# Roots of the query and key norms: from GpSimd's power and a three-round iteration to ten VectorE operations

## Chip, cores and metric

The kernel runs on one core of one Trainium2 chip. The metric is the device time of one execution in microseconds (us).

## What is computed

A transformer block for 16 sequences of 128 tokens with 128 features: a modulated linear layer, causal attention with 16 query heads and 4 key heads of 8 features (weights made ternary), a residual, an LSTM over the 128 tokens, a quantised feed-forward layer and a second residual. The part that the change touches is the root-mean-square norm of every query and key head:

```python
def rms_norm(x):
    eps = jnp.asarray(jnp.finfo(x.dtype).eps, x.dtype)
    return x * jax.lax.rsqrt(jnp.mean(x * x, axis=-1, keepdims=True) + eps)
...
q, k = (rms_norm(q), rms_norm(k))
...
q = q * q_gain.astype(q.dtype)[None, None, :, None]
...
x = x + _L0_attn_ref(_L0_cond_ref(x, cond_1024, L0_cond_weight), ...)
x = x + _L0_ffn_ref(_L0_cond2_ref(x, cond_1024, L0_cond2_Wx, L0_cond2_Wh, L0_cond2_b), ...)
```

## The kernel before

The 128 tokens of every sequence are cut into four blocks of 32 tokens. Attention goes block by block; the LSTM goes token by token, in 128 steps. The attention of block 0 and part of that of block 1 is done ahead of the LSTM's first step (the prologue); the rest of blocks 1 to 3 is spread over the steps by tables written by hand (`..._AT`, lines 392 to 434): step t of every engine ends with `side(t)`, which issues what the tables have for t. All engines run their own instruction list in order and wait for each other by counting semaphores.

One LSTM step is a ring: TensorE adds the products with the hidden state (line 1343), ScalarE takes tanh of the gates (line 958), VectorE makes the cell (`prod`, line 1846, and line 1849), ScalarE takes tanh of the cell (line 963), VectorE makes the hidden state in two parts (`h_hi`, line 1854, `h_lo`, line 1858), and TensorE begins the next step. VectorE's side work stands between `h_lo` of one step and `prod` of the next; TensorE's stands behind the products of the next step.

The norm of a block needs the sums of squares of 8 features for 80 columns (4 tiles of 20 heads) on 128 partitions (`sum_squares`, line 1562), and then 1/sqrt of mean plus epsilon, times the gain. It is made in two ways:

- Blocks 0 and 1, in the prologue, on VectorE (`head_norm`, lines 1564 to 1586): 13 operations, each of which waits for the one before: scale and epsilon, a shift and a subtraction on the bits as a first guess, three rounds of three operations, the gain.
- Blocks 2 and 3 on GpSimd (`head_norms`, lines 522 to 533): scale and epsilon, a power with exponent -0.5 (line 529), the gain. Block 2's stands between `row_norms(0)` and `max_parts(1, 0)`, block 3's between `max_parts(2, 1)` and `max_parts(2, 2)`.

`max_parts(k, u)` (lines 548 and 550) writes the maxima of the scores (`neg_max`, line 1632, VectorE) into the stack `m_stack`, from which TensorE's `lowered_queries` (lines 1088 and 1091) makes lowered queries; TensorE does so for tile 2 of block 2 in step 38. The roots are used by `scale_heads` (line 1609): in the prologue for blocks 0 and 1, in step 14 for block 2 and in step 46 for block 3.

In the prologue GpSimd makes identity and masks; it waits for VectorE (line 1708), takes the power for the modulation (line 566), makes the masks, fills the places of the values (`v_1`, which the trace names `v`, and `v_all`, lines 587 to 590), makes `gate_pick` and fills paddings. Behind VectorE's root of block 1 stand the ten operations of `ternary(PROJ_C, n)` (lines 1499 to 1523).

Of the kernel before, what the change touches and what calls it, by code (L numbers as in the profile page):

```python
# [23 lines left out]


def adaln_attention_lstm_ffn(nc, xT, condT, cond_w, w_qkv, w_proj, q_gain, Wx, Wh, b, clip_x,
# [4 lines left out]
    HD = D // HEADS  # L31
# [23 lines left out]
    with ExitStack() as ctx:  # L55
# [3 lines left out]
        def sem(name):  # L59
            return ctx.enter_context(nc.semaphore(name))  # L60
# [452 lines left out]
        def _(gp):  # L513
# [3 lines left out]
            def then(ins):  # L517
                made[0] += 1
                ins.then_inc(pool, 1)
                gp.wait_ge(pool, made[0])  # L520

            def head_norms(k):

                c, n = k % 2, QK_POOL_OPS * (k - 2)
                gp.wait_ge(squares_summed, 2 * k + 2)
                G.tensor_scalar(qk_r[:, c, 1, :], qk_r[:, c, 1, :], 1.0 / HD, FP32_EPS, ALU.mult, ALU.add).then_inc(qk_pool, 1)
                gp.wait_ge(qk_pool, n + 1)
                gp.wait_ge(rotated, 2 * (k - 1))
                G.tensor_tensor(qk_r[:, c, 0, :], qk_r[:, c, 1, :], minus_half[:, :].broadcast_to([P, TILES * NH]), ALU.pow).then_inc(qk_pool, 1)  # L529
                gp.wait_ge(qk_pool, n + 2)  # L530
                gp.wait_ge(gain_ready, 1)
                r = qk_r[:, c, 0, :].rearrange("p (t h) -> p t h", t=TILES)[:, :, 0:HEADS]
                G.tensor_tensor(r, r, gain_n[:, :].unsqueeze(1).broadcast_to([P, TILES, HEADS]), ALU.mult).then_inc(qk_pool, 1)

            def row_norms(k):
# [17 lines left out]
            def normalise_0(T):  # L553
# [31 lines left out]
            gp.wait_ge(masks, 1)  # L585

            then(G.memset(v_1[:, :, :, :], 0.0))
            then(G.memset(v_1[:, :, :, HD], 1.0))
            then(G.memset(v_all[:, :, :, :], 0.0))
            G.memset(v_all[:, :, :, HD], 1.0).then_inc(v_pads, 1)  # L590
# [408 lines left out]
        def _(pe):  # L999
# [465 lines left out]
        def _(v):  # L1465
# [98 lines left out]
            def head_norm(k, n):  # L1564


                c = k % 2
                x, y, tmp = qk_r[:, c, 1, :], qk_r[:, c, 0, :], qk_r[:, c, 2, :]
                if n == 0:
                    v.wait_ge(squares_summed, 2 * k + 2)  # L1570
                    V.tensor_scalar(x, x, 1.0 / HD, FP32_EPS, ALU.mult, ALU.add).then_inc(qk_link, 1)
                    return
                v.wait_ge(qk_link, QK_OPS * k + n)
                if n == 1:
                    V.tensor_scalar(tmp.bitcast(I32), x.bitcast(I32), 1, None, ALU.logical_shift_right).then_inc(qk_link, 1)
                elif n == 2:
                    V.tensor_scalar(y.bitcast(I32), tmp.bitcast(I32), -1.0, float(0x5F3759DF), ALU.mult, ALU.add).then_inc(qk_link, 1)
                elif n > NEWTON:
                    r = y.rearrange("p (t h) -> p t h", t=TILES)[:, :, 0:HEADS]
                    V.tensor_tensor(r, r, gain_n[:, :].unsqueeze(1).broadcast_to([P, TILES, HEADS]), ALU.mult).then_inc(qk_link, 1)  # L1580
                elif n % 3 == 0:
                    V.tensor_tensor(tmp, y, y, ALU.mult).then_inc(qk_link, 1)
                elif n % 3 == 1:
                    V.scalar_tensor_tensor(out=tmp, in0=tmp, scalar=-0.5, in1=x, op0=ALU.mult, op1=ALU.mult).then_inc(qk_link, 1)
# [17 lines left out]
            def scale_heads(k, h):  # L1602
                v.wait_ge(turned_qk, 2 * k + h + 1)
                if k < 2:
                    v.wait_ge(qk_link, QK_OPS * (k + 1))
                else:
                    v.wait_ge(qk_pool, QK_POOL_OPS * (k - 1))
# [179 lines left out]
            def side(t):  # L1787
# [3 lines left out]
                for k in range(1, BLOCKS):  # L1791
# [177 lines left out]
```

## Time and profile before

| what | us |
| --- | --- |
| median of 3 runs | 347.69 |
| the runs | 342.56, 348.14, 347.69 |
| span of the profiled execution | 345.6 |
| TensorE busy in it | 281.5 |
| VectorE busy | 230.0 |
| ScalarE busy | 179.6 |
| GpSimd busy | 71.8 |

The profiled execution has a span, from its first to its last instruction; its device time apart from the span isn't listed. The median lies 2.1 us above this span and the fastest run 3.0 us below it. The times of rows are us from the start of the span. A row of a timeline says: start, length, engine, line, operation, output <- input, shape; in brackets the idle time of the engine just before it, and what ended it.

### The profile page before, as it was taken

What the parts mean: (1) busy time and instruction counts of PE and PEld (TensorE: products, weight loads), DVE (VectorE), ACT (ScalarE), POOL (GpSimd) and SP (SyncE); (2) the same over time, 40 slices, a digit from 0 to 9 for tenths busy, and PEclk for the clock granted to TensorE, in tenths of its full rate; (3) what the DMA queues carried; (4) which work ended last, traced back from release to release, by engine and by line L of the source; (5) the groups of instructions that cost most, each with busy time, mean ns of one, the idle gap of its engine ahead of it and who ended that gap; (6) DMA issues with size and microseconds to landing.
All of it is one profiled execution on the core that took longest, in us unless ns stands there. A gap on an engine that the chain in (4) does not pass through costs nothing.

```text
span 345.6 us, 9250 instructions
## 1 busy us (share of the span) xinstructions
PE 281.5 (81%) x3509; PEld 175.5 (51%) x3510; DVE 230.0 (67%) x1077; ACT 179.6 (52%) x560; POOL 71.8 (21%) x95
## 2 busy tenths in 40 slices
PE   6949859898989789799988899997787887856243
PEld 2426544686757457576555676654444344321010
DVE  4686894758687777476578667545666565556866
ACT  7343953745466776556544555445225223249670
POOL 2731338700001039300020000001000000005624
PEclk9998996776598975555858756569999989996955
DMA  5600000000000000000000000000000000000003
GB/s 111 166 1 2 4 2 0 2 5 2 2 4 2 2 2 3 0 3 3 2 2 2 3 2 1 2 3 2 0 3 2 1 3 2 0 2 1 0 0 121
DMA packets 3773, 4.04 MB, mean 12 GB/s; under 512 B 1169, under 2 KB 2449, under 8 KB 3729
## 3 DMA queue, kind: packets, MB, share of 16 engines
q1 hardware_dynamic: 3360, 3.28, 3.5%
q8 instruction: 28, 0.46, 0.6%
q10 hardware_dynamic: 368, 0.16, 0.2%
q14 instruction: 17, 0.13, 0.1%
HBM read 2.40 MB, written 1.05 MB: 10 GB/s over the span
## 4 chain that ended last, share of the span: by engine, by line
PE 46%; DVE 26%; ACT 15%; issue 6%; POOL 4%; DMA 1%; ACTq 0%; DVEq 0%; POOLq 0%
PE bank L1343 14%; ACT tanh_c L963 4%; DVE prod L1846 4%; PE bank L1245 4%; PE bank L1407 4%; ACT gates_sb L958 4%; POOL qk_r L529 4%; DVE gates_sb L1849 4%; DVE h_hi L1854 4%; PE bank L1164 3%; PE bank L1252 3%; DVE neg_max L1632 2%; PE bank L1110 2%; PE bank L1199 2%; PE bank L1187 2%
## 5 line engine op out<-in xcount | busy, mean ns | idle before, releaser
L958 ACT ACTIVATE gates_sb<-bank 128x64 f32<-128x64 f32 x128 | 28.5, 223 | 73.3 <-PE bank L1343 70.9
L1343 PEld LDWEIGHTS bank<-h_hi,wh_hi 128*128 128x128 f16 x508 | 25.3, 103 | 71.5 <-DVE h_hi L1854 64.5
L1407 PE MATMUL bank<-ident_b,zero_w 128*128 128x512 bf16 x171 | 55.6, 422 | 0.0
L1846 DVE SCALAR_TENSOR_TENSOR prod<-gates_sb 128x32 f32<-128x32 f32 x128 | 24.7, 193 | 46.1 <-ACT gates_sb L958 43.2
L1343 PE MATMUL bank<-h_hi,wh_hi 128*128 128x16 f16 x508 | 34.4, 177 | 24.7 <-DVE h_hi L1854 24.0
L963 ACT ACTIVATE tanh_c<-gates_sb 128x16 f32<-128x16 f32 x128 | 27.6, 216 | 40.3 <-DVE gates_sb L1849 37.3
L1854 DVE TENSOR_TENSOR h_hi<-o_scaled,tanh_c 128x16 f16<-128x16 f32 x128 | 22.5, 176 | 25.3 <-ACT tanh_c L963 25.2
L1343 PE MATMUL bank<-h_lo,wh_hi 128*128 128x16 f16 x508 | 32.8, 174 | 0.1
L759 ACT ACTIVATE probs<-bank,gain_max 128x512 f32<-128x512 f32 (+1 forms) x44 | 29.4, 675 | 6.6 <-PE bank L1119 6.0
L1245 PE MATMUL bank<-x1T,wx_sb 128*128 128x128 f32 x128 | 32.2, 367 | 0.0
L1343 PE MATMUL bank<-h_hi,wh_lo 128*128 128x16 f16 x508 | 31.5, 171 | 0.0
L1632 DVE TENSOR_REDUCE neg_max<-bank 128x4 f32<-128x384 f32 (+3 forms) x44 | 27.7, 636 | 1.4 <-PE bank L1077 1.4
L529 POOL TENSOR_TENSOR qk_r<-qk_r,minus_half 128x80 f32<-128x80 f32 x2 | 26.2, 13106 | 0.2
L635 POOL TENSOR_TENSOR h_ffn<-xT_sb 96x512 f32<-96x512 f32 (+1 forms) x8 | 10.0, 1263 | 77.6 <-ACT xT_sb L985 77.6
L1858 DVE TENSOR_TENSOR h_lo<-hidden,h_hi 128x16 f16<-128x16 f32 x128 | 22.4, 175 | 4.4
L1849 DVE SCALAR_TENSOR_TENSOR gates_sb<-prod 128x16 f32<-128x16 f32 x128 | 22.4, 175 | 4.4
L1343 PEld LDWEIGHTS bank<-h_lo,wh_hi 128*128 128x128 f16 x508 | 22.0, 100 | 2.0 <-DVE h_lo L1858 0.2
L1252 PE MATMUL bank<-zero_w 128*128 128x512 bf16 x65 | 21.8, 493 | 1.2 <-DVE one L1688 1.2
L1245 PEld LDWEIGHTS bank<-x1T,wx_sb 128*128 128x128 f32 x128 | 22.5, 236 | 0.4 <-issue 0.4
L1343 PEld LDWEIGHTS bank<-h_hi,wh_lo 128*128 128x128 f16 x508 | 22.4, 99 | 0.0
L1856 DVE TENSOR_TENSOR hidden<-o_scaled,tanh_c 128x16 f32<-128x16 f32 x128 | 21.5, 168 | 0.1
L1851 DVE TENSOR_SCALAR o_scaled<-gates_sb 128x16 f32<-128x16 f32 x128 | 21.5, 168 | 0.0
(245 smaller groups left out, 520.6 us busy)
## 6 DMA issues: line engine op xcount, KB each, us to landing
xT_sb<-xT SPq DMA_DIRECT2D x4, 256.0 KB, 4.9
outT<-probs SPq DMA_DIRECT2D x4, 256.0 KB, 2.7
wh_sb<-Wh SPq DMA_DIRECT2D x1, 256.0 KB, 2.7
wx_sb<-Wx SPq DMA_DIRECT2D x1, 256.0 KB, 5.4
ffn_nat<-w_down SPq DMA_DIRECT2D x1, 176.0 KB, 3.6
ffn_nat<-w_gate SPq DMA_DIRECT2D x1, 128.0 KB, 3.7
ffn_nat<-w_up SPq DMA_DIRECT2D x1, 128.0 KB, 3.5
w_nat<-w_qkv ACTq DMA_DIRECT2D x1, 64.0 KB, 1.9
```

Of the source, the lines that this page charges most:

```text
L529: G.tensor_tensor(qk_r[:, c, 0, :], qk_r[:, c, 1, :], minus_half[:, :].broadcast_to([P, TILES * NH]), ALU.pow).then_inc(qk_pool, 1)
L759: A.activation(probs[0:keys, n % 2, g, :], bank[COL_BANKS[k][g]][0:keys, :], ACT.Exp, scale=gain_max[0:keys, 2:3]).then_inc(probs_ready, 1)
L958: A.activation(gates_sb[:, now, 0:GATES * B], bank[(t // BANK_STEPS) % 2][:, slot:slot + GATES * B], ACT.Tanh, scale=scale).then_inc(gates ...
L963: A.activation(tanh_c[:, :], gates_sb[:, nxt, GATES * B:], ACT.Tanh, scale=0.5).then_inc(tanh_done, 1)
L1245: return E.matmul(out, wx_sb[:, g * P:(g + 1) * P], x1T[:, chunk * BANK_STEPS:(chunk + 1) * BANK_STEPS, :], start=False, stop=False, skip_ ...
L1252: E.matmul(bank[dst][:, :], zero_w[:, :], zero_w[:, :].unsqueeze(1).broadcast_to([P, 4, P]), start=not keep, stop=not keep, skip_group_che ...
L1343: ins = E.matmul(bank[dst][:, col:col + B], w[:, g * P:(g + 1) * P], h[:, part, :], start=False, stop=True, skip_group_check=True)
L1407: E.matmul(bank[1 - ((t + 1) // BANK_STEPS) % 2][:, :], zero_w[:, :], ident_b[:, :].unsqueeze(1).broadcast_to([P, 4, P]), start=False, sto ...
L1632: V.tensor_reduce(neg_max[:, per * u:per * (u + 1), g], bank[ROW_BANKS[k][g]][:, 0:per * keys].rearrange("p (b k) -> p b k", b=per), AX.X, ...
L1846: V.scalar_tensor_tensor(out=prod[:, :], in0=G[:, now, 0:2 * B], scalar=1.0, in1=G[:, now, 3 * B:5 * B], op0=ALU.add, op1=ALU.mult).then_i ...
L1849: V.scalar_tensor_tensor(out=G[:, nxt, 4 * B:5 * B], in0=prod[:, B:2 * B], scalar=0.5, in1=prod[:, 0:B], op0=ALU.mult, op1=ALU.add).then_i ...
L1854: V.tensor_tensor(h_hi[:, now, :], o_scaled[:, :], tanh_c[:, :], ALU.mult).then_inc(hidden_hi, 1)
```

## The change

All four blocks take the root on VectorE with ten operations: one fewer for the first guess and two rounds instead of three, the second of them of higher order, with the gain multiplied in between (it waits for nothing new). Block 0 and block 1 do the ten in the prologue. Blocks 2 and 3 do two of the ten per LSTM step, block 2 in steps 0 to 4, block 3 in steps 33 to 37; `sum_squares` of block 3 stays in step 32. GpSimd's `head_norms` is gone. The four fills of `v_1` and `v_all` stand ahead of the power of the modulation; `gate_pick` gets a semaphore of its own.

```diff
+ROOT_A, ROOT_B, ROOT_S = 0.703952253, 2.38924456, 0.375
...
-        NEWTON = 11
-        QK_OPS = NEWTON + 2
-        QK_POOL_OPS = 3
+        QK_OPS = 10
...
+        NORMS_AT = {2: tuple(n // 2 for n in range(QK_OPS)), 3: tuple(33 + n // 2 for n in range(QK_OPS))}
...
-            def head_norms(k):
-
-                c, n = k % 2, QK_POOL_OPS * (k - 2)
-                gp.wait_ge(squares_summed, 2 * k + 2)
-                G.tensor_scalar(qk_r[:, c, 1, :], qk_r[:, c, 1, :], 1.0 / HD, FP32_EPS, ALU.mult, ALU.add).then_inc(qk_pool, 1)
-                gp.wait_ge(qk_pool, n + 1)
-                gp.wait_ge(rotated, 2 * (k - 1))
-                G.tensor_tensor(qk_r[:, c, 0, :], qk_r[:, c, 1, :], minus_half[:, :].broadcast_to([P, TILES * NH]), ALU.pow).then_inc(qk_pool, 1)
...
+            then(G.memset(v_1[:, :, :, :], 0.0))
+            then(G.memset(v_1[:, :, :, HD], 1.0))
+            then(G.memset(v_all[:, :, :, :], 0.0))
+            G.memset(v_all[:, :, :, HD], 1.0).then_inc(v_pads, 1)
             gp.wait_ge(demod_eps, 1)
             G.tensor_tensor(demod[:, 0, :], demod[:, 1, :], minus_half[:, :].broadcast_to([P, B]), ALU.pow).then_inc(demod_ready, 1)
...
-            head_norms(2)
             max_parts(1, 0)
...
-            head_norms(3)
             for u in range(2, UNITS[2]):
...
+                after = (0, 1, 2, 3, 4, 5, 6, 6, 7, 9)[n]
                 if n == 0:
                     v.wait_ge(squares_summed, 2 * k + 2)
...
+                else:
+                    v.wait_ge(qk_link, QK_OPS * k + after)
+                if n == 0:
+                    ins = V.tensor_scalar(x, x, 1.0 / HD, FP32_EPS, ALU.mult, ALU.add)
+                elif n == 1:
+                    ins = V.tensor_scalar(y.bitcast(I32), x.bitcast(I32), -0.5, float(0x5F1FFFF9), ALU.mult, ALU.add)
                 elif n == 2:
+                    ins = V.tensor_tensor(tmp, y, y, ALU.mult)
+                elif n == 3:
+                    ins = V.scalar_tensor_tensor(out=tmp, in0=tmp, scalar=-ROOT_A * ROOT_S, in1=x, op0=ALU.mult, op1=ALU.mult)
+                elif n == 4:
+                    ins = V.scalar_tensor_tensor(out=y, in0=tmp, scalar=ROOT_A * ROOT_B * ROOT_S, in1=y, op0=ALU.add, op1=ALU.mult)
+                elif n == 5:
+                    ins = V.scalar_tensor_tensor(out=tmp, in0=y, scalar=1.0 / (ROOT_S * ROOT_S), in1=y, op0=ALU.mult, op1=ALU.mult)
+                elif n == 6:
+                    ins = V.tensor_tensor(tmp, tmp, x, ALU.mult)
+                elif n == 7:
...
+                    ins = V.tensor_tensor(r, r, gain_n[:, :].unsqueeze(1).broadcast_to([P, TILES, HEADS]), ALU.mult)
+                elif n == 8:
+                    ins = V.scalar_tensor_tensor(out=tmp, in0=tmp, scalar=-10.0 / 3.0, in1=tmp, op0=ALU.add, op1=ALU.mult)
                 else:
+                    ins = V.scalar_tensor_tensor(out=y, in0=tmp, scalar=5.0, in1=y, op0=ALU.add, op1=ALU.mult)
+                ins.then_inc(qk_link, 1)
...
+                        for n in range(QK_OPS):
+                            if t == NORMS_AT[k][n]:
+                                head_norm(k, n)
```

GpSimd's list in the prologue, before, from the clearing of `diag_w` on (the masks follow it, and behind them the four fills of lines 587 to 590):

```order
L564 MEMSET diag_w 128x224
L566 TENSOR_TENSOR demod<-demod,minus_half 128x16
L570 AFFINE_SELECT diag_w<-diag_w 128x128 x4
L572 MEMSET mask_rows 128x32
L573 MEMSET mask_cols 128x32
```

And the same place after the change:

```order
L550 MEMSET diag_w 128x224
L551 MEMSET v 128x1024
L552 MEMSET v 128x32
L553 MEMSET v_all 128x2048
L554 MEMSET v_all 128x64
L556 TENSOR_TENSOR demod<-demod,minus_half 128x16
L560 AFFINE_SELECT diag_w<-diag_w 128x128 x4
L562 MEMSET mask_rows 128x32
L563 MEMSET mask_cols 128x32
```

The four fills have moved from behind the masks to the place ahead of the power of `demod`.

GpSimd's list from the maxima of block 2's second unit on, before:

```order
L550 TENSOR_TENSOR m_stack<-neg_max,m_stack 128x16
L526 TENSOR_SCALAR qk_r<-qk_r 128x80
L529 TENSOR_TENSOR qk_r<-qk_r,minus_half 128x80
L533 TENSOR_TENSOR qk_r<-qk_r,gain_n 128x4x16
L548 CAST m_stack<-neg_max 128x16
L550 TENSOR_TENSOR m_stack<-neg_max,m_stack 128x16
L548 CAST m_stack<-neg_max 128x16
L550 TENSOR_TENSOR m_stack<-neg_max,m_stack 128x16
L537 TENSOR_SCALAR rms_y<-y_sum 128x4
```

And after the change:

```order
L536 TENSOR_TENSOR m_stack<-neg_max,m_stack 128x16
L534 CAST m_stack<-neg_max 128x16
L536 TENSOR_TENSOR m_stack<-neg_max,m_stack 128x16
L534 CAST m_stack<-neg_max 128x16
L536 TENSOR_TENSOR m_stack<-neg_max,m_stack 128x16
L523 TENSOR_SCALAR rms_y<-y_sum 128x4
```

The three operations of block 3's root, the power among them, no longer stand between the second and the third unit's maxima.

VectorE's list at the end of LSTM step 3 and the start of step 4, before (`neg_max` is the side work of the step):

```order
L1858 TENSOR_TENSOR h_lo<-hidden,h_hi 128x16
L1632 TENSOR_REDUCE neg_max<-bank 128x8
L1846 SCALAR_TENSOR_TENSOR prod<-gates_sb 128x32
L1849 SCALAR_TENSOR_TENSOR gates_sb<-prod 128x16
L1851 TENSOR_SCALAR o_scaled<-gates_sb 128x16
```

And after the change:

```order
L1852 TENSOR_TENSOR h_lo<-hidden,h_hi 128x16
L1624 TENSOR_REDUCE neg_max<-bank 128x8
L1571 TENSOR_TENSOR qk_r<-qk_r 128x80
L1576 TENSOR_TENSOR qk_r<-qk_r,gain_n 128x4x16
L1840 SCALAR_TENSOR_TENSOR prod<-gates_sb 128x32
L1843 SCALAR_TENSOR_TENSOR gates_sb<-prod 128x16
L1845 TENSOR_SCALAR o_scaled<-gates_sb 128x16
```

Two operations of block 2's root stand between the side work of the step and `prod` of the next; the other nine pairs stand in the same place of their steps.

## Rows read from the trace of the kernel before

**Rows 1.** The page: clock by 40 slices; the chain by engine and line.
```profile
PEclk9998996776598975555858756569999989996955
...
PE 46%; DVE 26%; ACT 15%; issue 6%; POOL 4%; DMA 1%; ACTq 0%; DVEq 0%; POOLq 0%
```

**Rows 2.** Waits of TensorE, 20 to 60 us: total, times, longest.
```profile
PE bank L1056 <- DVE wmax L1738: 4.4, 1, 4.4
```

**Rows 3.** Timeline of VectorE, 15 to 26 us: block 0's root.
```profile
17.39 1.69 DVE L1571 TENSOR_SCALAR qk_r<-qk_r 128x80 f32<-128x80 f32 x1
...
22.17 0.23 DVE L1580 TENSOR_TENSOR qk_r<-qk_r,gain_n 128x64 f32<-128x64 f32 x1
22.65 0.89 DVE L1599 TENSOR_TENSOR rot<-rot,sin_part 128x320 f32<-128x320 f32 x2 [0.26 <-issue]
```

**Rows 4.** Timeline of POOL (GpSimd), prologue.
```profile
1.56 0.28 POOL L564 MEMSET diag_w<- 128x224 bf16 x1
7.48 2.96 POOL L566 TENSOR_TENSOR demod<-demod,minus_half 128x16 f32<-128x16 f32 x1 [5.63 <-DVE demod L1708]
...
15.99 0.95 POOL L587 MEMSET v<- 128x1024 f32 x1
...
17.22 1.80 POOL L589 MEMSET v_all<- 128x2048 f32 x1
19.08 0.20 POOL L590 MEMSET v_all<- 128x64 f32 x1
```

**Rows 5.** Timeline of VectorE, 36.7 to 44.7 us: block 1's root and what follows.
```profile
37.70 0.20 DVE L1571 TENSOR_SCALAR qk_r<-qk_r 128x80 f32<-128x80 f32 x1
...
38.41 0.24 DVE L1582 TENSOR_TENSOR qk_r<-qk_r 128x80 f32<-128x80 f32 x1
...
40.89 0.23 DVE L1580 TENSOR_TENSOR qk_r<-qk_r,gain_n 128x64 f32<-128x64 f32 x1
41.03 1.20 DVE L1499 CAST tw_b<-w_nat 128x128 bf16<-128x128 f32 x1
```

**Rows 6.** Timeline of POOL (GpSimd), later.
```profile
40.99 1.16 POOL L613 TENSOR_TENSOR wh_lo<-wh_sb,wh_hi 128x512 f16<-128x512 f32 x1 [2.70 <-ACT wh_hi L851]
...
53.45 13.11 POOL L529 TENSOR_TENSOR qk_r<-qk_r,minus_half 128x80 f32<-128x80 f32 x1
...
75.34 0.32 POOL L548 CAST m_stack<-neg_max 128x32 f16<-128x32 f32 x1 [8.39 <-DVE neg_max L1632]
...
127.56 13.11 POOL L529 TENSOR_TENSOR qk_r<-qk_r,minus_half 128x80 f32<-128x80 f32 x1
```

**Rows 7.** Timeline of PE (TensorE), 121 to 146 us: the wait in step 38.
```profile
141.67 0.60 PE L1088 MATMUL bank<-ident_h,q_stack 128*128 128x128 f16 x4 [1.75 <-POOL m_stack L550]
```

**Rows 8.** Timeline of VectorE in steps 1, 2, 4, 35 and 37.
```profile
63.26 0.42 DVE L1627 COPY qT<-bank 128x512 f16<-128x512 f16 x1
63.95 0.19 DVE L1846 SCALAR_TENSOR_TENSOR prod<-gates_sb 128x32 f32<-128x32 f32 x1 [0.27 <-ACT gates_sb L958]
...
67.61 0.19 DVE L1846 SCALAR_TENSOR_TENSOR prod<-gates_sb 128x32 f32<-128x32 f32 x1
...
131.55 0.19 DVE L1846 SCALAR_TENSOR_TENSOR prod<-gates_sb 128x32 f32<-128x32 f32 x1 [0.16 <-ACT gates_sb L958]
...
136.38 0.55 DVE L1632 TENSOR_REDUCE neg_max<-bank 128x4 f32<-128x384 f32 x1
```

**Rows 9.** Timeline of PE (TensorE), 0 to 64 us: products with zeros.
```profile
15.94 5.34 PE L1252 MATMUL bank<-zero_w 128*128 128x512 bf16 x24
...
27.22 1.48 PE L1252 MATMUL bank<-zero_w 128*128 128x512 bf16 x3
...
52.07 4.43 PE L1252 MATMUL bank<-zero_w 128*128 128x512 bf16 x10
```

**Rows 10.** Instructions of line 1846, 110 to 125 us and 126 to 139 us.
```profile
L1846 DVE SCALAR_TENSOR_TENSOR prod<-gates_sb x8: 191/192/194, 111.1 to 123.4; 128x32 f32<-128x32 f32 x8
...
L1846 DVE SCALAR_TENSOR_TENSOR prod<-gates_sb x6: 192/193/329, 127.6 to 137.1; 128x32 f32<-128x32 f32 x6
```

More of the change, by code:

```diff
@@ L211, in adaln_attention_lstm_ffn @@
         masks = sem("masks")
+        picks = sem("picks")
         pads = sem("pads")
@@ L237, in adaln_attention_lstm_ffn @@
         qk_link = sem("qk_link")
-        qk_pool = sem("qk_pool")
         cos_0 = sem("cos_0")
@@ L364, in adaln_attention_lstm_ffn @@
         Y_OPS = 2
-        NEWTON = 11
-        QK_OPS = NEWTON + 2
-        QK_POOL_OPS = 3
+        QK_OPS = 10
         PADS = 4 + TB
-        MASKS = 1 + PARTS
         LIN_BANKS = (4, 4, 4, 3)
@@ L520, in then @@
                 gp.wait_ge(pool, made[0])
-            def head_norms(k):
-                c, n = k % 2, QK_POOL_OPS * (k - 2)
-                gp.wait_ge(squares_summed, 2 * k + 2)
-                G.tensor_scalar(qk_r[:, c, 1, :], qk_r[:, c, 1, :], 1.0 / HD, FP32_EPS, ALU.mult, ALU.add).then_inc(qk_pool, 1)
-                gp.wait_ge(qk_pool, n + 1)
-                gp.wait_ge(rotated, 2 * (k - 1))
-                G.tensor_tensor(qk_r[:, c, 0, :], qk_r[:, c, 1, :], minus_half[:, :].broadcast_to([P, TILES * NH]), ALU.pow).then_inc(qk_pool, 1)
[L530 to L533, printed above, removed]
             def row_norms(k):
@@ L585, in _ @@
             gp.wait_ge(masks, 1)
[L587 to L590, printed above, removed]
             then(G.memset(gate_pick[:, :, :], 0.0))
@@ L593, in _ @@
                 G.affine_select(out=gate_pick[:, :, :], in_=gate_pick[:, :, :], compare_op=ALU.not_equal, fill=1.0,
-                                base=-GATES * part, pattern=[[-1, GATES], [0, B]], channel_multiplier=1).then_inc(masks, 1)
-                gp.wait_ge(masks, 2 + part)
+                                base=-GATES * part, pattern=[[-1, GATES], [0, B]], channel_multiplier=1).then_inc(picks, 1)
+                gp.wait_ge(picks, 1 + part)
             then(G.memset(ffn_nat[I_LAST:P, 0:2, (IC - 1) * P:IC * P], 1.0))
@@ L1313, in _ @@
             project_qkv(2, 1)
-            pe.wait_ge(masks, MASKS)
+            pe.wait_ge(picks, PARTS)
             pe.wait_ge(biasT_ready, 1)
@@ L1568, in head_norm @@
                 x, y, tmp = qk_r[:, c, 1, :], qk_r[:, c, 0, :], qk_r[:, c, 2, :]
+                after = (0, 1, 2, 3, 4, 5, 6, 6, 7, 9)[n]
                 if n == 0:
                     v.wait_ge(squares_summed, 2 * k + 2)
[L1571 to L1575, printed above, removed]
-                elif n == 2:
-                    V.tensor_scalar(y.bitcast(I32), tmp.bitcast(I32), -1.0, float(0x5F3759DF), ALU.mult, ALU.add).then_inc(qk_link, 1)
-                elif n > NEWTON:
-                    r = y.rearrange("p (t h) -> p t h", t=TILES)[:, :, 0:HEADS]
[L1580 to L1584, printed above, removed]
-                else:
-                    V.scalar_tensor_tensor(out=y, in0=tmp, scalar=1.5, in1=y, op0=ALU.add, op1=ALU.mult).then_inc(qk_link, 1)
@@ new lines, in head_norm @@
+                else:
[4 more added lines that the diff above has]
+                    ins = V.tensor_scalar(y.bitcast(I32), x.bitcast(I32), -0.5, float(0x5F1FFFF9), ALU.mult, ALU.add)
+                elif n == 2:
+                    ins = V.tensor_tensor(tmp, y, y, ALU.mult)
[8 more added lines that the diff above has]
+                elif n == 7:
+                    if k == 0:
+                        v.wait_ge(gain_ready, 1)
+                    r = y.rearrange("p (t h) -> p t h", t=TILES)[:, :, 0:HEADS]
+                    ins = V.tensor_tensor(r, r, gain_n[:, :].unsqueeze(1).broadcast_to([P, TILES, HEADS]), ALU.mult)
+                elif n == 8:
+                    ins = V.scalar_tensor_tensor(out=tmp, in0=tmp, scalar=-10.0 / 3.0, in1=tmp, op0=ALU.add, op1=ALU.mult)
+                else:
+                    ins = V.scalar_tensor_tensor(out=y, in0=tmp, scalar=5.0, in1=y, op0=ALU.add, op1=ALU.mult)
@@ L1603, in scale_heads @@
                 v.wait_ge(turned_qk, 2 * k + h + 1)
[L1604 to L1607, printed above, removed]
+                v.wait_ge(qk_link, QK_OPS * (k + 1))
                 n = half(h)
@@ L1728, in _ @@
             turn_sin_0()
-            v.wait_ge(gain_ready, 1)
             head_norms(0)
```

## The prediction

> **What bounds the kernel now.** I read the page first, then the waits of TensorE in the prologue, then the timelines of VectorE and GpSimd around the two kinds of root, and last TensorE's timeline where it waits for GpSimd. The page's chain runs through TensorE for 46% of the span and VectorE for 26%; GpSimd has 4%, about 14 us, which is one long piece of it [rows 1]. In the prologue VectorE is what is waited for: TensorE idles 4.4 us ahead of block 0's transposes until VectorE has come through its list [rows 2], and block 0's root stands in that list. In the LSTM steps the ring through four engines bounds the time; side work costs only where it outlasts the gap that the ring leaves on its engine. GpSimd's power takes 13.11 us twice [rows 6]. The second one is the 4% of the chain: TensorE stands still for 1.75 us in step 38 until the maxima queued behind that power are in `m_stack` [rows 7].
>
> **Price of one root operation.** Block 1's root shows them undisturbed: three scalar operations from 37.70 to 38.41, 0.24 us each from start to start; nine with two inputs from 38.41 to 40.89, 0.276 each; and the gain, behind which an operation that doesn't wait for it begins after 0.14 [rows 5]. Together 3.33 us from 37.70 to 41.03. The new ten: two scalar operations, 0.47; the four that make guess and square, 4 x 0.276 = 1.10; then the product with x (n = 6), in whose shadow the gain goes, 0.28; the next, 0.28; and 0.15 until the work behind the last can begin. That is 2.28, so an undisturbed root is 1.05 us shorter.
>
> One rule speaks against the short gaps. The row of the gain shows 0.23 us of length and the next start after 0.14 [rows 5]. The Trainium skill, "VectorE: DVE Perf Modes", section "The DRAIN you can't avoid", says that the next operation doesn't start until the pipe is empty, with or without a semaphore. By that rule the gain wouldn't hide and every pair in a step would cost about 0.1 us more, a microsecond in all; the row disagrees with it, and the sum goes by the row.
>
> **Block 0, on the path.** Here the first operation lasts 1.69 us instead of 0.20 [rows 3, 5]. It begins at 17.39, while GpSimd's fill of `v_all` runs from 17.22 to 19.02, and ends at 19.08, just behind that fill [rows 4]. The fills move to the front: `diag_w` ends at 1.84 and the power waits for VectorE until 7.48 [rows 4]; the four fills, which now run from 15.99 to 19.28 = 3.29 us, would end at about 5.1, with 2.3 us to spare, so the power isn't late. What GpSimd does at 17.4 then is `gate_pick` and paddings, short pieces. Root 0 lasts 5.26 from 17.39 to 22.65, 0.26 of it an idle piece with no releaser [rows 3]. After: 2.28, plus the idle piece, plus 0.2 for a short collision, is 2.74. Saved: 2.5. The bounds: 1.05 if something else on GpSimd holds the first operation as long as now, 2.98 if neither collision nor idle piece is left. I take the value near the upper one, as the fill that held it is gone. TensorE's wait of 4.4 us has room for all of it [rows 2].
>
> The row of the held operation ends 0.06 us behind the fill [rows 3, 4]. The Trainium skill, "SBUF — State Buffer", section "Who interferes with whom", says that VectorE's scalar operations can take a pair of ports shared with GpSimd, whoever comes second being blocked for the whole instruction. By this rule the 1.49 us over the undisturbed length go with the fill, as in the 2.5; without it the operation may be slow for a reason of its own, and 1.05 is left.
>
> **Block 1, on the path.** The root is 1.05 shorter. Behind it the cast of line 1499 takes 1.20, beginning at 41.03 beside GpSimd's `wh_lo`, 40.99 to 42.15 [rows 5, 6]. `wh_lo` follows ScalarE, whose work doesn't get shorter here, so VectorE comes to the cast a microsecond ahead of it. The cast goes through, and one of the next scalar operations, three to five places behind, meets `wh_lo` instead. I count the stall as moved, not gone: 1.0 saved in all, between 0.2 (a stall that is worse placed) and 2.0 (no stall left).
>
> **Block 2, steps 0 to 4.** Removing its power from GpSimd gives nothing: the maxima behind it wait 8.39 us for VectorE anyway [rows 6]. On VectorE a dependent pair costs 0.276 + 0.15 = 0.43, an independent one 0.29. In step 1 the gap behind the copy of `qT` is 0.27 idle [rows 8], so 0.16 shows; step 2 is like it. The pair of step 3 stands ahead of `prod` at 67.61, which has no idle before it [rows 8], so 0.29 shows at most; in steps 0 and 4 I find wider gaps. That is 0.6 on VectorE; TensorE has work of its own at that point and takes the state late anyway, so I count half, 0.3 (bounds 0 and 0.6).
>
> **Block 3, steps 33 to 37.** The power goes, and TensorE's 1.75 us go with it [rows 7]: the last maximum of that unit is made at 136.38 to 136.93 [rows 8], GpSimd's two short pieces take 0.6, and TensorE asks at 139.9. Even 1.0 us of delay in these steps leaves slack; the bound on the other side is 0.9, if half of the stall returns as a wait for `h_hi`. Against this, four of the five pairs follow a maximum, and step 35's `prod` comes after 0.16 idle [rows 8]: 3 x (0.43 - 0.16) + (0.29 - 0.16) = 0.94 on VectorE. TensorE runs at the lower of its levels there (below) and is the slower engine, so I count 0.4 (bounds 0 and 0.94).
>
> **The sum.** -2.5 - 1.0 + 0.3 - 1.75 + 0.4 = -4.55, about -4.6 us. The profiled span of 345.6 would become 341.0. What lies around the span isn't shown; the median of the runs is 2.1 above it, and I keep that: 347.69 - 4.6 = 343.1 us, 1.3% less. The measurement of this kernel can tell about 2% from no change; its three runs alone differ by 5.6 us.
>
> **The rivals.**
>
> *The clock stays up (faster).* The granted clock is near full in the first slices, dips in the fourth, and is 0.6 in the seventh [rows 1]. The same products with zeros cost 0.22 us each at 15.94, 0.49 at 27.22 and 0.44 at 52.07 [rows 9], so both later groups ran at or near 1.2 GHz and the first at 2.4 GHz. The dip at 27 follows the 4.4 us of idle TensorE [rows 2]; with the root 2.5 us earlier that idle time is 1.9. If neither dip comes, 3 x 0.27 + 10 x 0.22 = 3.0 us go as well: -7.6, 340.1 us. For it: the idle stretch more than halves. Against it: TensorE still has thin stretches ahead of 52, and the idle piece doesn't vanish.
>
> *The prologue's gain is hidden (same).* If TensorE's own zeros or ScalarE take over as the limit behind root 0, only step 38 pays: -1.75 + 0.7 = -1.05, 346.6 us. Against it: the 4.4 us [rows 2] and VectorE's list without an idle mark around root 1 [rows 5].
>
> *The pairs feed the low clock (slower).* A step takes (123.4 - 111.1)/7 = 1.76 us in the stretch before the clock falls and (137.1 - 127.6)/5 = 1.90 behind it [rows 10], in the four slices at 0.5 [rows 1]. If the pairs in steps 33 to 37 make TensorE wait for the state, so that it stays at 1.2 GHz through the rest of block 3's steps, each step costs 0.14 more. From 4.6/0.14 = 33 more low steps on the gain is gone; with 50 (steps 39 to 88) the time is 343.1 + 7.0 = 350.1 us. For it: the clock is already low for four slices here. Against it: a standstill of 1.75 us goes from the same stretch.
>
> **Chances.** Forecast 0.55, clock up 0.25, hidden 0.12, low clock 0.08. The forecast's own range is 340.9 to 345.1: with the better ends of all terms (0.5, 1.0 and 0.7) 2.2 us more go; with all worse ends (1.45, 0.8, 0.3, 0.54 and 0.9) 4.0 come back, of which I take half, since they don't come together. The wider range takes in the fast rival with the better ends, 340.1 - 2.2 = 337.9, and on the other side the hidden gain plus the 2.1 by which I set the median above the span, 348.7. Faster by over 2% means below 340.7: nearly all of the clock rival and a little of the forecast, 0.27. Slower by over 2% means above 354.6: 0.02. The rest, 0.71, lies within 2%.
>
> **What would show it.** Block 0's first root operation at 0.2 to 0.5 us instead of 1.69, and 2.3 to 2.8 us from it to the next line; the power of `demod` still at about 7.5 us; `prod` of step 1 at about 60.4 instead of 63.95 [rows 8]; the wait of TensorE for `m_stack` in step 38 gone; steps 33 to 37 within 0.2 us of what they take now. I am wrong if the first operation is still held, if step 1 starts less than 2 us earlier, if the pairs lengthen steps by 0.4 us and more, or if the clock's low slices move to where they cost more than the terms save.

## The result and the profile after

The changed kernel takes 334.49 us (median of 4 runs, 332.46 to 337.59); the kernel before, beside it on the same chip, 345.62 (342.56 to 348.14). The ratio is 0.9691, 95% interval 0.9595 to 0.9786: some 11 us less, where 4.6 were forecast, and below both ranges of the forecast (340.9 and, with the rivals, 337.9 at the fast end). Of 16 runs of the changed kernel in three sessions the median is 335.4, of 59 of the kernel before 345.6, so about 10 us is the gain to explain. Medians here are of all runs; ratios and their intervals are of the runs in the faster of two states alone. The profiled execution has a span of 333.5 us and a device time of 335.35; what lies around the span is 1.8 us.

The page of the changed kernel, the clock by 40 slices and the chain by engine:

```profile
PEclk9999958796997855556955775599999999995755
...
PE 46%; DVE 28%; ACT 16%; issue 6%; POOL 2%; DVEq 0%; ACTq 0%; POOLq 0%
```

Against [rows 1] GpSimd's share of the chain has halved, from 4% to 2%. The fourth slice stands at 9 instead of 8; the first low slice is the sixth, at 5, where it was the seventh, at 6. VectorE's two roots and what follows the second:

```profile
15.82 0.21 DVE L1559 TENSOR_SCALAR qk_r<-qk_r 128x80 f32<-128x80 f32 x1
...
17.59 0.22 DVE L1576 TENSOR_TENSOR qk_r<-qk_r,gain_n 128x64 f32<-128x64 f32 x1
17.73 0.23 DVE L1578 SCALAR_TENSOR_TENSOR qk_r<-qk_r 128x80 f32<-128x80 f32 x1
...
18.16 0.89 DVE L1594 TENSOR_TENSOR rot<-rot,sin_part 128x320 f32<-128x320 f32 x2
...
32.47 0.20 DVE L1559 TENSOR_SCALAR qk_r<-qk_r 128x80 f32<-128x80 f32 x1
...
34.77 0.22 DVE L1483 CAST tw_b<-w_nat 128x128 bf16<-128x128 f32 x1
...
36.08 1.07 DVE L1495 TENSOR_SCALAR tw_q<-tw_r 128x128 f32<-128x128 bf16 x1
```

Root 0 lasts 18.16 - 15.82 = 2.34 us where it lasted 5.26 [rows 3]; its first operation is at 0.21, and the idle piece of 0.26 behind the gain is gone too. It also begins 1.57 us earlier, at 15.82 instead of 17.39. That isn't the change's doing: in e1 below, the same changed kernel, it begins at 17.10, and in four other profiles with the old root at 15.64 to 16.19. Root 1 lasts 34.77 - 32.47 = 2.30 instead of 3.33 [rows 5]. The cast behind it takes 0.22 instead of 1.20, but the fifth operation behind the cast now takes 1.07: the collision with `wh_lo` has moved. GpSimd's timeline in the prologue shows that `wh_lo`, and the fills:

```profile
1.91 0.95 POOL L551 MEMSET v<- 128x1024 f32 x1
...
3.13 1.80 POOL L553 MEMSET v_all<- 128x2048 f32 x1
4.99 0.21 POOL L554 MEMSET v_all<- 128x64 f32 x1
7.26 3.09 POOL L556 TENSOR_TENSOR demod<-demod,minus_half 128x16 f32<-128x16 f32 x1 [2.06 <-DVE demod L1700]
...
35.77 1.29 POOL L599 TENSOR_TENSOR wh_lo<-wh_sb,wh_hi 128x512 f16<-128x512 f32 x1 [2.70 <-ACT wh_hi L835]
```

The fills are over at 5.20 and the power still waits 2.06 us for VectorE, so they cost nothing in front [rows 4]. VectorE's `prod` in steps 38 to 40, with the idle time ahead of it in brackets:

```profile
126.62 0.18 DVE L1840 SCALAR_TENSOR_TENSOR prod<-gates_sb 128x32 f32<-128x32 f32 x1
...
128.65 0.19 DVE L1840 SCALAR_TENSOR_TENSOR prod<-gates_sb 128x32 f32<-128x32 f32 x1 [0.39 <-ACT gates_sb L942]
...
130.71 0.19 DVE L1840 SCALAR_TENSOR_TENSOR prod<-gates_sb 128x32 f32<-128x32 f32 x1 [0.67 <-ACT gates_sb L942]
```

These two steps take 4.09 us. In the profile of before they take 6.21:

```profile
137.09 0.19 DVE L1846 SCALAR_TENSOR_TENSOR prod<-gates_sb 128x32 f32<-128x32 f32 x1 [0.17 <-ACT gates_sb L958]
...
143.30 0.19 DVE L1846 SCALAR_TENSOR_TENSOR prod<-gates_sb 128x32 f32<-128x32 f32 x1 [2.61 <-ACT gates_sb L958]
```

The wait for `m_stack` [rows 7] is gone. So far the forecast's places are right. What it left out shows in TensorE's waits between 18 and 30 us and in the ten products with zeros (timeline), behind which VectorE's copy of `ynT` waits:

```profile
PE bank L1040 <- DVE wmax L1729: 1.3, 1, 1.3
```

```profile
46.66 3.76 PE L1236 MATMUL bank<-zero_w 128*128 128x512 bf16 x10
```

```profile
50.90 0.42 DVE L1773 COPY ynT<-bank 128x256 f32<-128x256 f32 x1 [3.31 <-PE bank L1198]
```

The idle stretch ahead of block 0's transposes is 1.3 us instead of 4.4 [rows 2], and the clock no longer falls behind it. The ten products take 0.38 each, between the 0.22 of the upper level and the 0.44 that they took before [rows 9]; they hold up VectorE for 3.31 us, as they did before.

### The profile page after: what moved, and what is told of

The parts are those of the page before. It is cut to its first block, busy times and chain, and to the rows that moved or that the text cites. A ratio compares the mean times of both kernels' runs of the same rounds, so it can differ in the third digit from the quotient of the medians.

```text
span 333.5 us, 9253 instructions
## 1 busy us (share of the span) xinstructions
PE 275.4 (83%) x3509; PEld 170.3 (51%) x3510; DVE 229.1 (69%) x1091; ACT 180.1 (54%) x560; POOL 45.1 (14%) x89
## 4 chain that ended last, share of the span: by engine, by line
PE 46%; DVE 28%; ACT 16%; issue 6%; POOL 2%; DVEq 0%; ACTq 0%; POOLq 0%
PE bank L1327 15%; ACT tanh_c L947 5%; ACT gates_sb L942 4%; DVE prod L1840 4%; DVE h_hi L1848 4%; DVE gates_sb L1843 4%; PE bank L1148 4%; PE bank L1229 4%; PE bank L1391 4%; DVE neg_max L1624 2%; PE bank L1094 2%; PE bank L1103 2%; PE bank L1183 2%; PE bank L1057 2%; PE bank L1171 2%
## 5 line engine op out<-in xcount | busy, mean ns | idle before, releaser
L1229 PE MATMUL bank<-x1T,wx_sb 128*128 128x128 f32 x128 | 31.1, 357 | 0.0
L1229 PEld LDWEIGHTS bank<-x1T,wx_sb 128*128 128x128 f32 x128 | 21.8, 229 | 0.5 <-issue 0.5
L1391 PEld LDWEIGHTS bank<-ident_b,zero_w 128*128 128x128 bf16 x171 | 14.8, 102 | 13.1 <-issue 6.7
L1236 PE MATMUL bank<-zero_w 128*128 128x512 bf16 x65 | 18.6, 436 | 1.2 <-DVE one L1680 1.2
```

Of the source, the lines that this page charges most:

```text
L1229: return E.matmul(out, wx_sb[:, g * P:(g + 1) * P], x1T[:, chunk * BANK_STEPS:(chunk + 1) * BANK_STEPS, :], start=False, stop=False, skip_ ...
L1391: E.matmul(bank[1 - ((t + 1) // BANK_STEPS) % 2][:, :], zero_w[:, :], ident_b[:, :].unsqueeze(1).broadcast_to([P, 4, P]), start=False, sto ...
```

## The experiments

**One table for all runs.** In each profile I read five stretches from start times: root 0 (first operation to the next line); from its end to root 1's first operation; from the first `y_turn` to the first `prod`; steps 38 and 39 (`prod` to `prod`, counted from 0; the wait that the prediction puts into step 38 lies in them); steps 48 to 64 in the same way. "Idle" is TensorE's wait ahead of block 0's transposes. Times in us.

| run | median | idle | root 0 | to root 1 | to step 0 | 38, 39 | 48 to 64 |
| --- | --- | --- | --- | --- | --- | --- | --- |
| before | 345.6 | 4.4 | 5.26 | 15.05 | 15.86 | 6.21 | 32.31 |
| after | 334.5 | 1.3 | 2.34 | 14.31 | 15.80 | 4.09 | 33.46 |
| e1 after again | 335.6 | 1.7 | 2.47 | 14.34 | 12.62 | 4.09 | 33.98 |
| e2 fills only | 342.3 | 2.9 | 3.76 | 14.32 | 17.25 | 6.85 | 32.79 |
| e3 roots 0, 1 only | 339.8 | 2.1 | 2.83 | 14.42 | 15.75 | 6.27 | 31.68 |
| e4 roots 2, 3 only | 342.5 | 3.5 | 4.53 | 17.21 | 15.79 | 4.09 | 31.92 |
| f1 before, 38 zeros | 342.2 | 2.0 | 5.85 | 14.31 | 16.26 | 6.86 | 32.21 |
| f2 after, 12 zeros | 339.7 | 3.9 | 2.34 | 17.05 | 14.22 | 4.08 | 33.50 |
| f3 prologue's part | 341.5 | 1.5 | 2.33 | 14.33 | 15.83 | 6.91 | 33.15 |
| h1 the same again | 337.9 | 1.5 | 2.35 | 14.32 | 12.62 | 6.91 | 32.20 |
| h2 after, third | 335.8 | 1.5 | 2.35 | 14.32 | 15.63 | 4.09 | 33.44 |
| g1 block 2 on GpSimd | 336.3 | 1.5 | 2.36 | 14.31 | 14.22 | 4.09 | 33.43 |
| g2 block 3 on GpSimd | 336.5 | 1.5 | 2.36 | 14.31 | 14.21 | 6.90 | 31.23 |
| f4 after, waits filled | 334.0 | 1.5 | 2.36 | 14.32 | 12.63 | 4.09 | 33.48 |
| g3 filled, 2 and 3 on GpSimd | 334.6 | 1.5 | 2.35 | 14.32 | 12.62 | 6.27 | 32.30 |
| g4 after, 4 zeros late | 334.9 | 1.5 | 2.35 | 14.31 | 13.01 | 4.09 | 32.32 |
| h3 before, all zeros | 341.0 | 2.0 | 5.83 | 14.33 | 12.73 | 6.21 | 32.32 |
| h4 filled, 29 and 7 zeros | 333.3 | 0.5 | 2.35 | 14.32 | 12.63 | 4.09 | 34.00 |

**The parts of the change.** Theory A says that only the pieces read off the rows count, 6 us; theory B that low stretches of the clock go as well.

e1 runs the changed kernel again.

> The changed kernel once more. Theory A (the fixed pieces alone: the held first operation and the idle piece 1.9, two shorter roots 2.1, the wait in step 38 and what follows it 2.1, less 0.2 for the pairs): 6 us under the kernel before; then the 11 us of the first comparison were partly the luck of where the clock's low stretches fell. Theory B (the change also takes away low stretches of the clock as a rule): 10 to 11 us under it again.

335.63, ratio 0.977 (0.9723 to 0.9818): the gain is real and above A's. But its profile has no low clock ahead of step 0 at all, where the first profile of the same kernel has it from 43 to 49 us: the stretch to step 0 takes 12.62 us in one and 15.80 in the other. Part of the clock is chance: the same program gets it or not. Its 9.2 us by the medians and 7.9 by the ratio lie between A's 6 and B's 10 to 11.

e2 moves the four fills and nothing else.

```diff
+            then(G.memset(v_1[:, :, :, :], 0.0))
+            then(G.memset(v_1[:, :, :, HD], 1.0))
+            then(G.memset(v_all[:, :, :, :], 0.0))
+            G.memset(v_all[:, :, :, HD], 1.0).then_inc(v_pads, 1)
             gp.wait_ge(demod_eps, 1)
```

> The kernel before with the four fills ahead of the modulation's power, nothing else. Theory A: the first operation of block 0's root takes 0.2 instead of 1.69 us and the time falls by 1.5 to 1.9 us. Theory B: 1 us or more on top, since TensorE's idle stretch ahead of block 0's transposes gets shorter too. Rival: the hold comes from something else, then the operation stays at 1.7 us and the time stays.

Root 0 falls from 5.26 to 3.76, by the 1.5 us of the held operation. The median is 342.25, 2.6 under the kernel before beside it, but its six runs go from 334.3 to 344.0, too wide for a price of 1.5 us. VectorE's timeline shows the first operation and the idle piece, which stays with the 13 operations:

```profile
16.15 0.19 DVE L1571 TENSOR_SCALAR qk_r<-qk_r 128x80 f32<-128x80 f32 x1
...
19.91 0.90 DVE L1599 TENSOR_TENSOR rot<-rot,sin_part 128x320 f32<-128x320 f32 x2 [0.26 <-issue]
```

e3 takes the ten operations for blocks 0 and 1 and leaves fills, blocks 2 and 3 as they were; e4 does blocks 2 and 3 alone.

```diff
-        NEWTON = 11
-        QK_OPS = NEWTON + 2
+        QK_OPS = 10
...
+                after = (0, 1, 2, 3, 4, 5, 6, 6, 7, 9)[n]
```

> The kernel before with the ten operations for blocks 0 and 1 alone; fills and GpSimd's powers stay. Theory A: two roots of 2.3 instead of 3.3 us and the first operation still held 1.7 us: 2.1 us less. Theory B: 3 us or more less.

> The kernel before with blocks 2 and 3 alone on VectorE, two operations per step; the prologue as before. Theory A: the wait for m_stack in step 38 goes (step 39 about 2.0 instead of 4.0 us), the pairs cost 0.2: 1.9 us less. Theory B: 4 us or more less, because the standstill kept the clock low behind it. Rival: the pairs cost 0.4 per step, then no gain.

e3: 339.78, ratio 0.9833 (0.9765 to 0.99); root 0 at 2.83. Its first operation is held for 0.73 by the short fill; the third, which would meet the long one, has two inputs now and runs on at 0.24. Its median is 5.0 us under the kernel before, so above theory A's 2.1. e4: 342.52, 2.3 us under the kernel before, ratio 0.9975 (0.9929 to 1.002), so not told from no change; steps 38 and 39 at 4.09. Its prologue ran at the lower level from 23 to 32 us, and the stretch to root 1 took 17.21. A's 1.9 us fit this, B's 4 don't.

**What holds a root operation.** In f1 (below) the old root meets both fills. VectorE's and GpSimd's timelines:

```profile
16.19 0.74 DVE L1571 TENSOR_SCALAR qk_r<-qk_r 128x80 f32<-128x80 f32 x1
...
17.20 1.80 DVE L1577 TENSOR_SCALAR qk_r<-qk_r 128x80 int32<-128x80 int32 x1
```

```profile
15.93 0.95 POOL L587 MEMSET v<- 128x1024 f32 x1
...
17.14 1.81 POOL L589 MEMSET v_all<- 128x2048 f32 x1
```

Each of these two scalar operations (`TENSOR_SCALAR`, one input) begins within a fill and ends 0.05 us behind it, at 16.93 and 19.00. e3 shows the other kind beside the same fill, VectorE and then GpSimd:

```profile
17.03 0.24 DVE L1579 TENSOR_TENSOR qk_r<-qk_r 128x80 f32<-128x80 f32 x1
```

```profile
16.97 1.80 POOL L589 MEMSET v_all<- 128x2048 f32 x1
```

Eight operations with two inputs follow each other there at 0.22 to 0.24 each. Having one input isn't what does it: in the kernel before, the two sums of squares, which also have one, run beside the fill from 15.99 to 16.94 [rows 4] and take 0.86, as in the changed kernel, where no fill runs then:

```profile
16.20 0.86 DVE L1562 TENSOR_REDUCE qk_r<-sq 128x40 f32<-128x320 f32 x2
```

The Trainium skill, "SBUF — State Buffer", section "Who interferes with whom", says that such scalar operations can take the pair of ports shared with GpSimd, while one with two inputs contends only with a GpSimd instruction that reads. The rows agree as far as they go: the scalar operations are held, and those with two inputs aren't held by a fill, which reads nothing. Whether a reading GpSimd instruction holds them, these rows don't show. So the old root lost 0.8 to 2.1 us here, as the fills happened to fall (4.53 to 5.85 in four profiles).

**The idle stretch ahead of block 0's transposes.** Theory C says that it brings the clock down for what follows; theory D that the level there is chance. f1 shortens it in the kernel before, f2 lengthens it in the changed one; nothing else moves.

```diff
-            idle(24, 7)
+            idle(38, 7)
```

> The kernel before with 38 instead of 24 products with zeros behind the second modulation's products, so that TensorE's 4.4 us of idling ahead of block 0's transposes shrink to about 1.3 us; nothing on VectorE's or GpSimd's path changes. Theory C (the idle stretch brings the clock down behind it, and a shorter stretch keeps it up): the low clock between 26 and 32 us goes, block 0's root to block 1's root takes 14.3 to 14.6 us instead of 15.1 (before) or 17.2 (the run with the late roots alone), and the time falls by 0.7 to 2.9 us. Theory D (the clock's level there is chance): a profile as before, no change of the time within 1 us.

> The changed kernel with 12 instead of 24 of these zero products: TensorE idles for about 3.9 us ahead of block 0's transposes instead of 1.3, with VectorE's path as it is. Theory C: the low clock behind block 0's transposes comes back, neg_max of block 0 and block 1's root start 0.7 to 2.9 us later, and the time rises by as much, to 336.3 to 338.5. Theory D: 335.6, as the changed kernel.

f1: 342.18, ratio 0.9913 (0.9876 to 0.995), 3.4 us less than before beside it by the medians and 1.7 to 4.3 by the interval. f2: 339.73, ratio 0.9882 (0.9807 to 0.9956), 4.1 us above the changed kernel on the same chip (e1); the intervals of these two touch. TensorE in windows of 6 us (window, its length, busy time and count, granted clock, share of the DMA and its GB/s). Before:

```profile
20.00:26.00 6.00, 1.55 (x11) 1.00 0.01 1
26.00:32.00 6.00, 6.00 (x102) 0.72 0.01 3
```

f1, the kernel before with 38 zeros:

```profile
20.00:26.00 6.00, 3.99 (x31) 1.00 0.00 1
26.00:32.00 6.00, 5.01 (x98) 1.00 0.01 3
```

f2, the changed kernel with 12:

```profile
20.00:26.00 6.00, 4.76 (x91) 0.50 0.01 3
26.00:32.00 6.00, 6.00 (x43) 0.64 0.00 0
```

The changed kernel:

```profile
20.00:26.00 6.00, 4.27 (x99) 1.00 0.01 3
26.00:32.00 6.00, 5.07 (x110) 1.00 0.00 0
```

Between these transposes and root 1 the granted clock is at the upper level (1.00) where TensorE idled 0.5 to 2.9 us (15 profiles), and fell to the lower one where it idled 3.5 to 4.4 (before, e4, f2). The stretch to root 1 takes 14.31 to 14.42 there and 15.05 to 17.21 here. C holds: in f2 the root ends as early as in the changed kernel, and root 1 begins 2.75 us later (35.22 against 32.47). The number of zeros alone doesn't decide it: with the same 24 of them the clock stays up in e3 (2.1 idle) and e2 (2.9) and falls in e4 (3.5) and before (4.4). Both medians moved by more than the 0.7 to 2.9 us that C expected, and the stretch to root 1 itself shows only 0.74 (before against f1) to 2.9 (e4 against f1); where the rest of the 3.4 and 4.1 falls, one profile of each can't tell.

**The ten products ahead of step 0.** f4 puts zeros into TensorE's two waits for VectorE there, g4 takes six of the ten away.

```diff
             modulate(2)
+            idle(4, 3)
             pe.wait_ge(tern_ready, 2)
...
             modulate(3)
+            idle(8, 2)
             project_qkv(2, 0)
```

> The changed kernel with four products with zeros behind the third modulation's product and eight behind the fourth's, where TensorE waits 1.0 and 2.0 us for VectorE. Theory C: the low clock that the profile of the changed kernel has from 43 to 49 us, where ten products with zeros take 3.76 us on the path, stays away; step 0 starts up to 3.2 us earlier than 53.97, and the time falls by 1.5 to 3 us, to 332.6 to 334.1. Theory D: no change; and if the zeros themselves run at the low clock they delay what follows by up to 2 us.

> The changed kernel with four instead of ten products with zeros ahead of the turning of block 0 into rows. In its profile these ten run at the low level and end 3.3 us after what VectorE and ScalarE have ready for TensorE. Theory C2 (the zeros themselves are on the path when the clock is low): up to 2.4 us go where it is low, so the time falls by 1 to 2 us, to 333.6 to 334.6. Rival: the six zeros that are missing make the clock fall later, in the first steps, and the time stays at 335.6 or rises.

f4: 334.0 (332.23 to 335.11), ratio 0.9692 (0.9636 to 0.9749). TensorE's zeros and VectorE's copy in it:

```profile
45.31 2.32 PE L1236 MATMUL bank<-zero_w 128*128 128x512 bf16 x10
```

```profile
48.18 0.42 DVE L1775 COPY ynT<-bank 128x256 f32<-128x256 f32 x1 [0.24 <-PE bank L1198]
```

The ten run at 0.23 each and hold VectorE up for 0.24. g4: 334.94, ratio 0.9656 (0.96 to 0.9712); its stretch to step 0 is 13.01 although the clock falls there. They are 1.6 and 0.7 us under e1 (g4 on another chip); the intervals of the ratios overlap for f4, and g4's lies just below e1's. With the waits filled the stretch is 12.62 to 12.73 in all four profiles (f4, g3, h3, h4); without, with all ten zeros, it is 12.62 in two of 13 (e1, h1) and 14.2 to 17.3 in the others.

h3 asks what zeros alone do for the kernel before, h4 whether f4 can be had better.

> The kernel before with zero products alone in TensorE's three waits of the prologue: 38 instead of 24, and eight each behind the third and the fourth modulation's products. It asks how much of the gain is the clock's and can be had without the change. Theory C: the 3.3 us of the 38 and 1.5 to 3 us of the late ones, 340.5 to 342 where before is 346; all fixed pieces (root 0, root 1, step 39) as in the kernel before.

> The run with the filled waits once more, with 29 instead of 24 and seven instead of ten zero products: the idle stretch ahead of block 0's transposes goes nearly to nothing and the zeros on the path get shorter. If those two still cost anything: 333 or less. If not: 334.0, as that run.

h3: 341.02, ratio 0.9858 (0.977 to 0.9946): 4.5 us by the medians, 1.9 to 7.9 by the interval, without any of the change. h4: 333.34 (332.17 to 334.73), ratio 0.9687 (0.9622 to 0.9751), against 335.8 for the changed kernel beside it (h2, 0.9694, 0.9614 to 0.9773). It is the fastest median here, though its interval doesn't part it from f4 or the changed kernel. h3 and h4, on one chip, show what the change is worth where zeros hold the clock up to step 0 in both kernels (their counts differ: 38, 8, 8 and ten in h3, 29, 4, 8 and seven in h4): 7.7 us by the medians, 5.9 by the ratios, where before and h2, without such zeros, lie 9.7 and 10.6 apart.

**The roots in the steps.** f3 is the changed kernel with blocks 2 and 3 back on GpSimd, g1 and g2 with one of them, g3 is f3 with f4's zeros. f3, h1 and g3 also take the old shared semaphore for `gate_pick`.

```diff
+            head_norms(3)
             for u in range(2, UNITS[2]):
...
+                            if k != ON_POOL and t == NORMS_AT[k][n]:
```

> The changed kernel with the roots of blocks 2 and 3 back on GpSimd (three operations each, the power among them): the prologue's part alone. Theory A (fixed pieces alone): 2.1 us of the wait in steps 38 and 39 come back, 0.2 us of pairs go, and it lies 4.1 us under the kernel before, 340.8. Theory B (low stretches of the clock go with the earlier prologue): it lies 1.9 us above the changed kernel, 337.5. The wait of TensorE in step 38 is back in both.

> The changed kernel with block 2's root alone back on GpSimd (three operations, the power among them), block 3's on VectorE. Both theories: the pairs of steps 0 to 4 go (0.2 us) and nothing waits for the power, so 335.4, within 1 us of the changed kernel; step 39 stays at 2.06 us.

> The changed kernel with block 3's root alone back on GpSimd, block 2's on VectorE. Fixed pieces: steps 38 and 39 take 2.21 and 4.0 to 4.7 us again instead of 2.03 and 2.06, the pairs of steps 33 to 37 go (0.15 us), so 2.0 to 2.7 us above the changed kernel, 337.6 to 338.3. Rival: the standstill of TensorE also shifts the clock's low stretches, and the time goes to 340 or more, as where both blocks are on GpSimd (341.5).

> The changed kernel with the twelve zero products of the run with the filled waits (334.0), and blocks 2 and 3 back on GpSimd. It asks the question of the step part again where the prologue holds the clock. Fixed pieces: 2.0 to 2.7 us above that run, 336.0 to 336.7. Rival (the power on GpSimd or the standstill brings more low clock): 339 or more.

f3: 341.47, ratio 0.9831 (0.9737 to 0.9926); g1: 336.31, 0.971 (0.9643 to 0.9776); g2: 336.53, 0.9735 (0.9679 to 0.9792); g3: 334.61, 0.966 (0.9604 to 0.9717). Block 2's move isn't told from nothing, as expected. Block 3's wait in steps 38 and 39 costs 2.1 to 2.8 us in every profile that has it, and yet by the medians g2 lies only 1 us above the changed kernel and g3 0.6 above f4, each on another chip; by the ratios g2 (0.9735) lies within the changed kernel's three (0.9691 to 0.977), and g3 (0.966) lies below f4 (0.9692). Part of it may come back in steps 48 to 64. TensorE in them, one window, in the changed kernel:

```profile
147.86:181.32 33.46, 30.68 (x377) 0.65 0.01 2
```

And in g2:

```profile
148.83:180.06 31.23, 27.68 (x378) 0.81 0.01 2
```

The same instructions take 33.46 us at 0.65 and 31.23 at 0.81 (the count differs by one record). Over the profiles these steps take 31.2 to 33.2 with block 3 on GpSimd and 33.4 to 34.0 without, e4 and g4 (31.9 and 32.3) apart. But the steps behind them partly undo this: from step 48 to the `prod` of the last step the profiles take 144.9 to 148.1 us with block 3 on GpSimd and 146.3 to 147.9 without, and the kernel before and after 146.8 and 147.2. So a loss in these steps is shown for steps 48 to 64 of most profiles, not for the whole, and its cause (the pairs or the lack of a standstill) wasn't tried.

f3's 341.5 didn't fit, so it ran again beside the changed kernel:

> The prologue's part alone, once more, beside the changed kernel on one chip. If the fixed pieces and the idle stretch add up, it is 1 to 2.7 us above the changed kernel (the steps' part), 337 to 338.5. If 341.5 comes again, the steps' part and the prologue's part don't add up, and the place of the clock's low stretches in the steps decides.

> The changed kernel for a third time, as the other end of that comparison: 335.6, as before.

h1: 337.87, ratio 0.9747 (0.9646 to 0.9849); h2: 335.8. The 2.1 us between the medians lie within what was expected (1 to 2.7), but the two intervals overlap. f3 and h1 are one program: its runs go from 335.9 to 343.9 and from 333.8 to 342.3, so f3's median can be chance. What the steps' part is worth in the whole run stays open: 2.3 us by e4's median, 2.1 by h1 and h2, about 1 or nothing by g2 and g3.

## Why the prediction was wrong

- **Block 0: right, a little small.** -2.5 forecast, -2.92 in the profiles. The held operation (1.5, e2) and the shorter root are as worked out; the idle piece of 0.26, which I kept, goes with the old form of block 0's root (it stays in e2 and isn't there in e3), and the 0.2 for a collision wasn't there. Its signs came as named: 0.21, 2.34, the power at 7.26.
- **Block 1: right.** -1.0 forecast, 3.33 - 2.30 = 1.03 found, and the stall "moved, not gone", from the cast to an operation five places on; only 0.14 of it went.
- **Pairs: right for block 2, too dear for block 3.** +0.3 and +0.4 forecast; steps 0 to 3 take 7.36 against 7.18 (+0.2; 7.05 to 7.25 in the other profiles without pairs there), steps 33 to 37 take 9.52 against 9.49, and against 9.35 to 9.51 in the other profiles with the power. The section of the Trainium skill that the prediction sets against its short gaps, "VectorE: DVE Perf Modes", "The DRAIN you can't avoid", also says that a next operation that isn't held starts earlier. So the row of the gain and that section need not disagree: here too the operation behind the gain starts 0.14 after it (17.59 and 17.73).
- **Step 38: right in place, open in what it is worth.** -1.75 forecast, 6.21 - 4.09 = 2.12 found. Steps 48 to 64 then take 33.46 - 32.31 = 1.15 more, and the steps from there to the last `prod` 0.73 less, so that this pair of profiles loses 0.4 behind step 47. The medians leave 0.6 to 2.3 us for it or, by the ratios, nothing that is told from chance.
- **The step that failed: the sum puts TensorE's clock at nothing.** It adds pieces of VectorE's and GpSimd's rows and leaves the clock behind the idle stretch as it was, though its own block 0 term cuts that stretch to less than half. The fixed pieces found are -2.92 - 1.03 - 0.14 - 2.12 + 0.18 + 0.03 = -6.0 us, against -4.55 worked out; some 4 of the 10 us are not in them. What the runs show in its place is the clock: zeros alone take 3.4 us (1.7 to 4.3) from the kernel before in f1, and f2 gives 4.1 back in the changed one. -6.0 with f1's interval is -7.7 to -10.3, which takes in the 10 measured. h3 and h4 say the same from the other side: with the clock held in both kernels the change is worth 5.9 to 7.7 us, near the 6.6 of the fixed pieces between their profiles (3.48 + 1.03 + 0.13 + 2.12 - 0.18 - 0.02), so that 2.0 to 4.7 of the 9.7 to 10.6 go with the clock. These are estimates; the parts were not measured in one run.
- **What was chance.** Of the 12.1 us between the spans of the two profiles the fixed pieces are 6.0 and the stretch to root 1 0.74. Root 0's earlier start is 1.57, which e1 doesn't have. Another 3.6 (3.42, and the 0.18 that the pairs cost) lie in the first 16 steps, which take 30.9 and 35.5 us in two profiles of one program (h1, f3). So this one pair of profiles shows the size of the clock's part poorly; the runs above do.
- **The rival "the clock stays up"** had the right cause and the right idle time (1.9 forecast, 1.3 found), but the wrong price and chance. It priced only the zeros, 0.8 us for the three at 27 us and 2.2 for the ten at 52. The first is too little, because the attention's products behind the idle stretch run at the lower level too: the stretch to root 1 takes 0.74 to 2.9 us longer where it is low, and f1's median shows 3.4. The second mostly didn't come, since the ten still run low in the changed kernel's first profile. And 0.25 was too little for it: rows 1 and 2 showed a dip of the clock right behind an idle time that the forecast itself cut to less than half.
- "The prologue's gain is hidden" is out: the `prod` that stood at 63.95 [rows 8] (step 2's, counted from 0; the prediction calls it step 1's) starts at 57.56, 6.4 earlier where 3.5 were forecast, and 4.8 without the 1.57 of root 0's earlier start. Slower steps all through ("the pairs feed the low clock") didn't come; steps 48 to 64 alone were slower, as said.

## What to carry to other kernels

When an edit shortens TensorE's idle stretch, read the granted clock behind that stretch and price everything that runs at the lower level there, not only the idle time; a run with filler products in the old kernel (f1, h3) gives that price before the edit is made. Filler products paid here where they stood in waits (f1, h3); as the last thing ahead of a result they are on the path, and dear when the clock is low already (ten of them held up VectorE for 3.31 us). A stall taken out of the steps need not shorten the run by its length: add up the steps behind it to the end, not only the stretch where the clock changes. And profile the same program twice before you read a difference of some us off one pair of profiles.

## What the runs showed of the hardware

- A scalar operation of VectorE (`TENSOR_SCALAR`) that begins within a GpSimd fill ends 0.05 to 0.06 us behind the fill, however late it began (0.73 to 1.80 us instead of 0.20; before, e3, e4, f1, h3). Operations with two inputs beside the same fill keep their 0.24, and a `TENSOR_REDUCE` with one input keeps its 0.86.
- Behind an idle time of 0.5 to 2.9 us the clock stayed at the upper level up to root 1 (15 profiles), behind 3.5 to 4.4 it fell to the lower one (before, e4, f2), whether 12 or 24 zeros stood ahead of it.
- One and the same program runs the stretch to step 0 in 12.62 or 15.80 us (e1 and the first profile of the changed kernel), by where the clock's low stretch falls. Its first 16 steps can differ by 4.6 us (30.86 in h1, 35.45 in f3): 2.5 of it lie in steps 4 to 6, where the values' products run at 1.00 in h1 and the granted clock is 0.61 in f3, and 1.6 in step 15.
